# A residual graph layer on one core: the gate as w + p·d, the last weights split early, and the last row tile in two column pieces

## The chip, the core and the metric

The kernel runs on one core of a Trainium2 chip. The time is the device time of one execution in microseconds (us), and the median of the runs is compared. The engines run side by side and wait for each other by semaphores only: PE multiplies matrices, ACT and DVE work on rows of 128 partitions, POOL does so more slowly, and SP issues the DMAs.

## The reference

625 nodes with 1024 features, 20000 edges of 8 types. The first layer is a graph attention (a product with W, softmax-like weights over the edges, elu), added to x and normalized. The second layer is relational: a product with a root matrix and, per type, a product of the mean of the neighbours with that type's weights. Its result u then gates the layer:

```python
u = _rgcn(x, edge_index, edge_type, weight, root, bias)
z = jnp.concatenate([u, x], axis=1) @ w_gate + b_gate
h = jnp.tanh(u) * z + x * (1.0 - z)
return h
...
x = _layernorm(x + _L1_gnn_ref(x, ...), axis=-1)
```

With the residual, what is normalized is 2x + z·(tanh(u) − x), where z is b_gate, plus x times the lower half of w_gate, plus u times its upper half.

## The kernel before

Rows of nodes are cut into 5 row tiles of 128 (the last has 113), the 1024 features into 8 blocks k of 128 and 2 halves of 512 columns. Each product of 32-bit numbers is made of three matmuls: both operands are split into a high part (f32r) and a low rest, and hi·hi, lo·hi and hi·lo are summed in PSUM (`product_item`, L924; lines 927 to 929). A weight chunk is 128 x 512. SP loads it into a ring of four buffers `w_raw` (L294), ACT casts the high part (L459), POOL subtracts for the low part (L393). A half product, called a segment here, takes 8 chunks. The segments run in one order; `SEG_G` (22) and `SEG_G + 1` (23) are the last two, the left and right half of u times the upper half of w_gate.

Up to segment 22 the chunks are the outer loop and the row tiles the inner one, so all five tiles become ready together. Meanwhile u is turned: PE transposes it (L1119), ACT takes the high part (`turned_u`, L606) and DVE the low part (L879). Segment 23 is different: its weights are written whole into the memory of the operand `M_hi[0]`, `M_lo[0]`, which is free once segment 21 is done (`last_w`, L142). There the row tiles are the outer loop (L1140), and each tile is ready after its 24 matmuls. The names: `last_chunk(k)` is chunk k of segment 23, on ACT (L598, L602) and on POOL (L396, L398).

z holds b_gate plus the part of x already. xf is x rebuilt from its two parts, by POOL (L434). ACT makes tanh(u) in place, after each of the first five last chunks (L628). POOL subtracts xf from it (`minus_x`, L405). DVE then does, for a half of a tile (`gate`, L884): z += product in PSUM (L887), z *= u (L890), u = 2·xf + z (L891), and the statistics of the columns (L892). It does so for the five tiles of half 0, then for half 1; after a tile's half 1 it combines the statistics (L899), ACT takes the root (L631), DVE the reciprocal (L901) and the scaling (L902), and SP stores the tile (L369, L373). Most DVE instructions carry a semaphore and wait for it themselves (`step`, L639).

The order on every engine is the order in which the code is written; no scheduler moves anything. PE waits for each chunk's low part in tile 0 (L1146), and from tile 3 on for the PSUM bank that DVE has to drain (L1142).

## Time and profile before

| | |
|---|---|
| timed runs | 1111.9, 1112.72, 1115.48 us (median 1112.72) |
| profiled execution | 1117.14 us |
| its span, first to last instruction | 1115.3 us |
| busy over the span | PE 1040.4 us, DVE 353.3, ACT 264.0, POOL 265.4 |
| chain that ended last, by engine | PE 83%, DVE 7%, POOL 3% |
| loads of a weight chunk | 192 of 256 KB, 2.9 us each from issue to landing |

The busy times are sums over the whole span. The change touches only the last 75 us or so, so the profile is read there: first the stretches between the borders of segments (segment 22 from 1039.00 to 1068.49 us, segment 23 from there to 1107.26), then the timelines of single engines. The start times are us from the span's start. ACT, DVE and POOL overlap the end of an instruction with the start of the next a little. The granted clock of PE is given as a share of 2.4 GHz.

### The profile page before, as it was taken

To read this page: it belongs to the slowest core of one execution; us is meant where nothing else is said; L and a number is where in the kernel's file an instruction comes from. 1 tells how busy PE (TensorE), PEld (TensorE's weight loads), DVE (VectorE), ACT (ScalarE), POOL (GpSimd) and SP (SyncE) were. 2 spreads that over 40 slices of the span, in tenths; PEclk is the share of its full clock that TensorE was granted. 3 is DMA by queue.
4 is the path that set the end of the run, shared out by engine and by line. 5 is a ranking of instruction groups with operands and counts; after the bars stand their busy time and mean duration, and the time that the engine had idled before them with its cause. 6 is when DMAs were issued, how large, how long until landed. Compare 5 with 4: busy or idle time off the path is not lost.

```text
span 1115.3 us, 14888 instructions
## 1 busy us (share of the span) xinstructions
PE 1040.4 (93%) x5432; PEld 861.0 (77%) x5432; DVE 353.3 (32%) x698; ACT 264.0 (24%) x452; POOL 265.4 (24%) x201
## 2 busy tenths in 40 slices
PE   5699878896999999999999999999999999999977
PEld 3455545585788889889889889889889889888855
DVE  7954566446111022022022022022012012112277
ACT  3212234345111121121121121122121122222320
POOL 0000000103532222222222312321311321327480
PEclk9989989998999999999999999999999999999988
DMA  6113323425622132132131131131141141212212
GB/s 207 48 57 114 95 58 87 153 80 191 179 79 64 38 108 65 39 115 59 38 121 52 38 123 51 38 125 48 38 135 39 38 135 38 76 48 66 76 39 92
DMA packets 63621, 91.81 MB, mean 82 GB/s; under 512 B 4115, under 2 KB 30178, under 8 KB 63428
## 3 DMA queue, kind: packets, MB, share of 16 engines
q1 hardware_dynamic: 63556, 90.86, 25.8%
q8 instruction: 51, 0.84, 0.3%
q14 instruction: 14, 0.11, 0.0%
HBM read 75.17 MB, written 15.67 MB: 81 GB/s over the span
## 4 chain that ended last, share of the span: by engine, by line
PE 83%; DVE 7%; POOL 3%; issue 2%; ACT 1%; DVEq 1%; POOLq 0%; ACTq 0%
PE ps L927 17%; PE ps L928 17%; PE ps L929 17%; PE ps L1098 9%; PE ps L1099 9%; PE ps L993 4%; PE ps L1087 2%; PE ps L956 2%; DVE hot L761 2%; POOL x_lo L420 1%; PE ps L1147 1%; POOL u L405 1%; PE ps L1148 1%; PE ps L1149 1%; DVE oh_s L699 1%
## 5 line engine op out<-in xcount | busy, mean ns | idle before, releaser
L393 POOL TENSOR_TENSOR w_lo<-w_raw,w_hi 128x512 fp32r<-128x512 f32 x168 | 215.3, 1285 | 771.0 <-ACT w_hi L459 553.6
L927 PE MATMUL ps<-w_hi,M_hi 128*128 128x512 f32 (+1 forms) x560 | 223.5, 399 | 17.7 <-DVE w_lo L694 11.4
L459 ACT CAST w_hi<-w_raw 128x512 fp32r<-128x512 f32 x184 | 114.2, 622 | 480.0 <-PE ps L929 415.3
L928 PE MATMUL ps<-w_hi,M_lo 128*128 128x512 f32 (+1 forms) x560 | 220.3, 393 | 0.0
L929 PE MATMUL ps<-w_lo,M_hi 128*128 128x512 f32 (+1 forms) x560 | 220.2, 393 | 0.0
L842 DVE SCALAR_TENSOR_TENSOR u<-ps,scale,u 128x512 f32<-128x512 f32 (+1 forms) x90 | 66.4, 744 | 423.1 <-PE ps L929 423.1
L1098 PE MATMUL ps<-C_hi,x_hi 128*128 128x320 f32 (+3 forms) x640 | 193.1, 319 | 0.0
L1099 PE MATMUL ps<-C_hi,x_lo 128*128 128x320 f32 (+3 forms) x640 | 192.0, 317 | 0.0
L927 PE MATMUL ps<-w_hi,M 128*128 128x512 f32 (+1 forms) x360 | 140.5, 390 | 0.0
L929 PE MATMUL ps<-w_lo,M 128*128 128x512 f32 (+1 forms) x360 | 140.5, 390 | 0.0
L928 PE MATMUL ps<-w_hi,M 128*128 128x512 f32 (+1 forms) x360 | 140.4, 390 | 0.0
L927 PEld LDWEIGHTS ps<-w_hi,M_hi 128*128 128x128 f32 (+1 forms) x560 | 105.1, 188 | 43.2 <-DVE w_lo L694 13.6
L1099 PEld LDWEIGHTS ps<-C_hi,x_lo 128*128 128x128 f32 (+1 forms) x640 | 127.5, 199 | 0.3
L1098 PEld LDWEIGHTS ps<-C_hi,x_hi 128*128 128x128 f32 (+1 forms) x640 | 127.3, 199 | 0.4
L929 PEld LDWEIGHTS ps<-w_lo,M_hi 128*128 128x128 f32 (+1 forms) x560 | 105.0, 188 | 23.7
L928 PEld LDWEIGHTS ps<-w_hi,M_lo 128*128 128x128 f32 (+1 forms) x560 | 105.3, 188 | 22.4
L761 DVE TENSOR_SCALAR hot<-table,key 128x640 bf16<-128x640 f16 x210 | 69.9, 383 | 70.1 <-PE ps L993 53.9
L993 PE MATMUL ps<-hot,oh_s 128*128 128x320 bf16 x420 | 76.0, 313 | 13.3 <-DVE hot L761 6.3
L929 PEld LDWEIGHTS ps<-w_lo,M 128*128 128x128 f32 (+1 forms) x360 | 66.7, 185 | 14.9
L928 PEld LDWEIGHTS ps<-w_hi,M 128*128 128x128 f32 (+1 forms) x360 | 66.8, 186 | 14.6
L927 PEld LDWEIGHTS ps<-w_hi,M 128*128 128x128 f32 (+1 forms) x360 | 66.8, 185 | 14.5
L993 PEld LDWEIGHTS ps<-hot,oh_s 128*128 x420 | 31.0, 99 | 46.4 <-issue 39.1
(140 smaller groups left out, 768.8 us busy)
## 6 DMA issues: line engine op xcount, KB each, us to landing
w_raw<-weights SPq DMA_DIRECT2D x192, 256.0 KB, 2.9
C_dram<-Cst SPq DMA_DIRECT2D x25, 512.0 KB, 5.9
C_hi<-C_dram SPq DMA_DIRECT2D x8, 1600.0 KB, 6.9
z<-b_gate SPq DMA_DIRECT2D x5, 512.0 KB, 9.6
u<-bias SPq DMA_DIRECT2D x5, 512.0 KB, 8.5
xT_raw<-xT SPq DMA_DIRECT2D x8, 312.5 KB, 7.5
u<-x SPq DMA_DIRECT2D x4, 512.0 KB, 5.0
out<-u SPq DMA_DIRECT2D x4, 512.0 KB
```

The source lines that it names most:

```text
L393: pool.tensor_tensor(w_lo[k % RING][:, :], w_raw[k % RING][:, :], w_hi[k % RING][:, :].bitcast(f32), ALU.subtract).then_inc(w_lo_done, 1)
L459: nc.scalar.copy(w_hi[k % RING][:, :], w_raw[k % RING][:, :]).then_inc(w_hi_done, 1)
L761: v.tensor_scalar(hot[:, SLOT[s] * NP:(SLOT[s] + 1) * NP], table[:, :], float(WIN * w), key[:, ds(tile + s, 1)], ALU.add, ALU.is_equal).th ...
L842: v.scalar_tensor_tensor(u[r, t, half * H2:(half + 1) * H2], bank(t, rows(t)), scale[odd][r, t:t + 1], u[r, t, half * H2:(half + 1) * H2], ...
L927: mm(o, lhs_hi[:, k, c], w_hi[k % RING][:, :], start=opens, stop=False)
L928: mm(o, lhs_lo[:, k, c], w_hi[k % RING][:, :], start=False, stop=False)
L929: last = mm(o, lhs_hi[:, k, c], w_lo[k % RING][:, :], start=False, stop=closes_)
L956: last = mm(bank(turn_bank(j, part), c0=(m - m0) * P, c=P), Cst[j % 2][:, m, r, :], ident_r[:, :], start=r == 0, stop=r == R - 1)
L993: last = mm(bank(5 + c, c=SPLIT), oh_s[:, ds(edge + s * P, P)], hot[:, SLOT[s] * NP + c * SPLIT:SLOT[s] * NP + (c + 1) * SPLIT], start=Fal ...
L1087: last = mm(bank(5, c0=2 * t, c=2), C_hi[:, m, t * P:(t + 1) * P], ones_r[:, 0:2], start=m == 0, stop=m == NT - 1)
L1098: mm(o, x1_hi[r, m, f], C_hi[r, m, c0:c0 + cn], start=m == 0, stop=False)
L1099: last = mm(o, x1_lo[r, m, f], C_hi[r, m, c0:c0 + cn], start=False, stop=m == NT - 1)
```

## The change

It has three parts.

First, the gate is written as w + p·d, with p the product in PSUM, d = tanh(u) − xf and w = 2·xf + z·d. DVE makes d in place of u and w in place of z, over 1024 columns at a time and before the gate's product is there (`gate_rest`); POOL's `minus_x` is gone. What is left per half tile is one multiplication that reads PSUM and one addition, which also sums its result. In tiles 0 to 3 the variance no longer comes from `bn_stats`: DVE makes the negative mean, ACT squares the deviations over 1024 columns with a sum (z only takes the squares), and then takes the root.

Second, the last weights are loaded and split earlier. The memory of x1_lo lies now, with that of C_hi, where xf and four buffers `last_raw` come, so chunks 0 to 3 of segment 23 have their own buffers; 4 to 7 still use the ring. They have semaphores of their own, and ACT and POOL take them between the last chunks of segment 22.

Third, the last row tile is multiplied in two pieces of 256 columns into two banks. DVE treats that tile in four quarters of 256 columns with `bn_stats`.

```diff
+            with ExitStack() as agg:
+                C_hi = sb("C_hi", [P, NT, NP], f32r, agg)
+                space = sb("space", [P, NT * (D - NP)], f32, agg)
+                x1_lo = sb("x1_lo", [P, NT, D], f32r, agg)
...
             xf = sb("xf", [P, NT, D], f32, late)
+            last_raw = [sb(f"last_raw{k}", [P, H2], f32, late) for k in range(RING)]
+            space2 = sb("space2", [P, NT * D - RING * H2], f32, late)
+            u = sb("u", [P, NT, D], f32, late)
+            z = sb("z", [P, NT, D], f32, late)
+            x1_hi = sb("x1_hi", [P, NT, D], f32r, late)
...
+        def raw_of_last(k):
+            return (last_raw[k] if k < RING else w_raw[k % RING])[:, :]
...
-            for n in range(SEG_U + 2 * R, SEG_G + 2):
-                load_ahead(n, last=n == SEG_G + 1)
+            for n in range(SEG_U + 2 * R, SEG_G + 1):
+                load_ahead(n, last=n == SEG_G)
+            sp.wait_ge(xf_done, NT)
+            for k in range(KT):
+                if k >= RING:
+                    sp.wait_ge(w_lo_done, 8 * SEG_G + k + 1)
+                r0, c0 = chunk_rows(SEG_G + 1, k)
+                sp.dma_start(raw_of_last(k), weights[ds(r0, P), c0:c0 + H2]).then_inc(last_here[k], 16)
...
             def last_chunk(k):
-                pool.wait_ge(w_hi_done, 8 * (SEG_G + 1) + k + 1)
-                pool.tensor_tensor(last_w(1, k), w_raw[k % RING][:, :], last_w(0, k).bitcast(f32),
-                                   ALU.subtract).then_inc(w_lo_done, 1)
-
-            def minus_x(t):
-                r = slice(0, rows(t))
-                pool.wait_ge(tanh_done, t + 1)
-                pool.wait_ge(xf_done, t + 1)
-                pool.tensor_tensor(u[r, t, :], u[r, t, :], xf[r, t, :], ALU.subtract).then_inc(d_done, 1)
+                pool.wait_ge(last_hi_done, k + 1)
+                pool.tensor_tensor(last_w(1, k), raw_of_last(k), last_w(0, k).bitcast(f32),
+                                   ALU.subtract).then_inc(last_lo_done, 1)
...
-            for k in range(KT):
-                if k < RING:
-                    split_chunk(SEG_G, k + RING)
-                else:
-                    last_chunk(k - RING)
-                if k >= KT - NT:
-                    minus_x(k - KT + NT)
-            for k in range(RING, KT):
+            split_chunk(SEG_G, RING)
+            last_chunk(0)
+            split_chunk(SEG_G, RING + 1)
+            last_chunk(1)
+            split_chunk(SEG_G, RING + 2)
+            last_chunk(2)
+            last_chunk(3)
+            split_chunk(SEG_G, RING + 3)
+            for k in range(4, KT):
                 last_chunk(k)
...
-                act.wait_ge(raw_here[k % RING], 32 * (SEG_G + 1) + 16 * (k // RING) + 16)
+                act.wait_ge(last_here[k], 16)
                 if k == 0:
                     act.wait_ge(u_ready, filled(SEG_G - 1))
-                nc.scalar.copy(last_w(0, k), w_raw[k % RING][:, :]).then_inc(w_hi_done, 1)
+                nc.scalar.copy(last_w(0, k), raw_of_last(k)).then_inc(last_hi_done, 1)
+
+            def tanh(t):
+                nc.scalar.activation(u[0:rows(t), t, :], u[0:rows(t), t, :], ACT.Tanh).then_inc(tanh_done, 1)
...
-            for kh in range(2):
-                n = SEG_G - 1 + kh
-                split_chunk(n, RING)
-                for t in range(GB):
-                    turned_u(t, kh)
-                split_chunk(n, RING + 1)
-                for t in range(GB, NT):
-                    turned_u(t, kh)
-                for k in range(RING + 2, KT):
-                    split_chunk(n, k)
-                if kh == 0:
-                    for k in range(RING):
-                        split_chunk(n + 1, k)
-            for k in range(KT):
+            split_chunk(SEG_G - 1, RING)
+            for t in range(GB):
+                turned_u(t, 0)
+            split_chunk(SEG_G - 1, RING + 1)
+            for t in range(GB, NT):
+                turned_u(t, 0)
+            for k in range(RING + 2, KT):
+                split_chunk(SEG_G - 1, k)
+            for k in range(RING + 1):
+                split_chunk(SEG_G, k)
+            for t in range(GB):
+                turned_u(t, 1)
+            last_chunk(0)
+            split_chunk(SEG_G, RING + 1)
+            for t in range(GB, NT):
+                turned_u(t, 1)
+            last_chunk(1)
+            tanh(0)
+            tanh(1)
+            split_chunk(SEG_G, RING + 2)
+            last_chunk(2)
+            tanh(2)
+            last_chunk(3)
+            tanh(3)
+            split_chunk(SEG_G, RING + 3)
+            last_chunk(4)
+            tanh(4)
+            for k in range(5, KT):
                 last_chunk(k)
-                if k < NT:
-                    act.wait_ge(uT_lo_done, 2 * NT)
-                    nc.scalar.activation(u[0:rows(k), k, :], u[0:rows(k), k, :], ACT.Tanh).then_inc(tanh_done, 1)
-            for t in range(NT):
-                act.wait_ge(var_done, t + 1)
-                nc.scalar.activation(rstd[0:rows(t), t:t + 1], mv[0:rows(t), t, 1:2], ACT.Sqrt,
-                                     bias=eps_col[0:rows(t), :]).then_inc(std2_done, 1)
+            for t in range(NT - 1):
+                r = slice(0, rows(t))
+                act.wait_ge(h_mean_done, t + 1)
+                nc.scalar.activation(z[r, t, :], u[r, t, :], ACT.Square, bias=h_neg_mean[r, t:t + 1],
+                                     accum_out=h_sq[r, t:t + 1]).then_inc(h_sq_done, 1)
+                act.wait_ge(h_sq_done, t + 1)
+                nc.scalar.activation(rstd[r, t:t + 1], h_sq[r, t:t + 1], ACT.Sqrt, bias=eps_col[r, :], scale=1.0 / D)\
+                  .then_inc(std2_done, 1)
+            r = slice(0, rows(NT - 1))
+            act.wait_ge(var_done, 1)
+            nc.scalar.activation(rstd[r, NT - 1:NT], mv[r, NT - 1, 1:2], ACT.Sqrt, bias=eps_col[r, :]).then_inc(std2_done, 1)
...
+            def gate_rest(t):
+                r = slice(0, rows(t))
+                dve.wait_ge(tanh_done, t + 1)
+                dve.wait_ge(xf_done, t + 1)
+                step(v.tensor_tensor(u[r, t, :], u[r, t, :], xf[r, t, :], ALU.subtract))
+                step(v.tensor_tensor(z[r, t, :], z[r, t, :], u[r, t, :], ALU.mult))
+                step(v.scalar_tensor_tensor(z[r, t, :], xf[r, t, :], 2.0, z[r, t, :], ALU.mult, ALU.add))
+
             def gate(t, half, from_bank):
                 r, c = slice(0, rows(t)), slice(half * H2, (half + 1) * H2)
                 dve.wait_ge(u_ready, NT * (SEG_G + half) + t + 1)
-                v.tensor_tensor(z[r, t, c], bank(from_bank, rows(t)), z[r, t, c], ALU.add).then_inc(u_drained, 1)
+                v.tensor_tensor(u[r, t, c], bank(from_bank, rows(t)), u[r, t, c], ALU.mult).then_inc(u_drained, 1)
                 dve.wait_ge(u_drained, NT * (SEG_G + half) + t + 1 + NT)
-                dve.wait_ge(d_done, t + 1)
-                step(v.tensor_tensor(z[r, t, c], z[r, t, c], u[r, t, c], ALU.mult))
-                step(v.scalar_tensor_tensor(u[r, t, c], xf[r, t, c], 2.0, z[r, t, c], ALU.mult, ALU.add))
-                step(v.bn_stats(stats[r, t, half, :], u[r, t, c]))
+                step(v.scalar_tensor_tensor(u[r, t, c], u[r, t, c], 1.0, z[r, t, c], ALU.mult, ALU.add,
+                                            accum_out=h_sum[r, t, half:half + 1]))
+
+            quarters = stats[:, 0:2, :, :].rearrange("p a b s -> p (a b) s")
+
+            def gate_quarter(q, from_bank, from_col):
+                t = NT - 1
+                r, c = slice(0, rows(t)), slice(q * Q, (q + 1) * Q)
+                at = NT * SEG_G + NT if q < 2 else NT * SEG_G + 2 * NT + q - 2
+                dve.wait_ge(u_ready, at)
+                step(v.tensor_tensor(u[r, t, c], bank(from_bank, rows(t), c0=from_col, c=Q), u[r, t, c], ALU.mult))
+                step(v.tensor_tensor(u[r, t, c], u[r, t, c], z[r, t, c], ALU.add))
+                step(v.bn_stats(quarters[r, q, :], u[r, t, c]))
+
+            def normalized(t, mean, op):
+                r = slice(0, rows(t))
+                dve.wait_ge(std2_done, t + 1)
+                step(v.reciprocal(rstd[r, t:t + 1], rstd[r, t:t + 1]))
+                v.tensor_scalar(u[r, t, :], u[r, t, :], mean, rstd[r, t:t + 1], op, ALU.mult).then_inc(y2_done, 1)
 
             for t in range(NT):
+                gate_rest(t)
+            for t in range(NT - 1):
                 gate(t, 0, t)
-            for t in range(NT):
+            for q in range(2):
+                gate_quarter(q, NT - 1, q * Q)
+            dve.sem_inc(u_drained, 1)
+            for t in range(NT - 1):
                 r = slice(0, rows(t))
                 gate(t, 1, last_bank(t))
-                v.bn_aggr(mv[r, t, :], stats[r, t, :, :]).then_inc(var_done, 1)
-                dve.wait_ge(std2_done, t + 1)
-                step(v.reciprocal(rstd[r, t:t + 1], rstd[r, t:t + 1]))
-                v.tensor_scalar(u[r, t, :], u[r, t, :], mv[r, t, 0:1], rstd[r, t:t + 1], ALU.subtract, ALU.mult)\
-                    .then_inc(y2_done, 1)
+                v.tensor_scalar(h_neg_mean[r, t:t + 1], h_sum[r, t, 1:2], h_sum[r, t, 0:1], -1.0 / D, ALU.add, ALU.mult)\
+                 .then_inc(h_mean_done, 1)
+                normalized(t, h_neg_mean[r, t:t + 1], ALU.add)
+            r = slice(0, rows(NT - 1))
+            for q in range(2, 4):
+                gate_quarter(q, last_bank(NT - 1) + q - 2, 0)
+            v.bn_aggr(mv[r, NT - 1, :], quarters[r, :, :]).then_inc(var_done, 1)
+            normalized(NT - 1, mv[r, NT - 1, 0:1], ALU.subtract)
...
-                c, o = slice(t * P, t * P + rows(t)), bank(last_bank(t), rows(t))
-                for k in range(KT):
-                    if t == 0:
-                        pe.wait_ge(w_lo_done, 8 * (SEG_G + 1) + k + 1)
-                    mm(o, M_hi[1][:, k, c], last_w(0, k), start=k == 0, stop=False)
-                    mm(o, M_lo[1][:, k, c], last_w(0, k), start=False, stop=False)
-                    last = mm(o, M_hi[1][:, k, c], last_w(1, k), start=False, stop=k == KT - 1)
-                last.then_inc(u_ready, 1)
+                c = slice(t * P, t * P + rows(t))
+                pieces = [(0, H2)] if t < NT - 1 else [(0, Q), (Q, H2)]
+                for f0, f1 in pieces:
+                    if f0 > 0:
+                        pe.wait_ge(u_drained, NT * SEG_G + t - GB + 2 + NT)
+                    o = bank(last_bank(t) + (f0 > 0), rows(t), c=f1 - f0)
+                    for k in range(KT):
+                        if t == 0:
+                            pe.wait_ge(last_lo_done, k + 1)
+                        mm(o, M_hi[1][:, k, c], last_w(0, k)[:, f0:f1], start=k == 0, stop=False)
+                        mm(o, M_lo[1][:, k, c], last_w(0, k)[:, f0:f1], start=False, stop=False)
+                        last = mm(o, M_hi[1][:, k, c], last_w(1, k)[:, f0:f1], start=False, stop=k == KT - 1)
+                    last.then_inc(u_ready, 1)
```

**ACT around the last chunks.** Before; w_hi is a chunk of segment 22, M_hi<-w_raw a last chunk, M<-ps a turned tile of u:

```order
289 L459 CAST w_hi<-w_raw 128x512 [waits w_used,raw_here1]
290 L606 CAST M<-ps 128x4x128 [waits uT_ready]
291 L606 CAST M<-ps 128x4x113 [waits uT_ready]
292 L459 CAST w_hi<-w_raw 128x512 [waits w_used,raw_here2]
293 L459 CAST w_hi<-w_raw 128x512 [waits w_used,raw_here3]
294 L602 CAST M_hi<-w_raw 128x512 [waits u_ready,raw_here0]
295 L628 ACT_TABLE_LOAD
296 L628 ACTIVATE u<-u 128x1024 [waits uT_lo_done]
```

and after the change:

```order
289 L617 CAST M_hi<-last_raw 128x512 [waits u_ready,last_here0]
290 L474 CAST w_hi<-w_raw 128x512 [waits w_used,raw_here1]
291 L624 CAST M<-ps 128x4x128 [waits uT_ready]
292 L624 CAST M<-ps 128x4x113 [waits uT_ready]
293 L617 CAST M_hi<-last_raw 128x512 [waits last_here1]
294 L620 ACT_TABLE_LOAD
295 L620 ACTIVATE u<-u 128x1024 x2
296 L474 CAST w_hi<-w_raw 128x512 [waits w_used,raw_here2]
297 L617 CAST M_hi<-last_raw 128x512 [waits last_here2]
```

The table load and the first tanh stood behind all of segment 22's chunks and stand now behind chunk 5, ahead of chunk 6.

**POOL around the last chunks.** Before; w_lo is a chunk of segment 22, M_lo a last chunk:

```order
96 L393 TENSOR_TENSOR w_lo<-w_raw,w_hi 128x512 [waits w_hi_done] x7
97 L405 TENSOR_TENSOR u<-u,xf 128x1024 [waits xf_done,tanh_done]
98 L398 TENSOR_TENSOR M_lo<-w_raw,M_hi 128x512 [waits w_hi_done]
99 L405 TENSOR_TENSOR u<-u,xf 128x1024 [waits xf_done,tanh_done]
100 L398 TENSOR_TENSOR M_lo<-w_raw,M_hi 128x512 [waits w_hi_done]
101 L405 TENSOR_TENSOR u<-u,xf 128x1024 [waits xf_done,tanh_done]
102 L398 TENSOR_TENSOR M_lo<-w_raw,M_hi 128x512 [waits w_hi_done]
```

and after:

```order
97 L418 TENSOR_TENSOR M_lo<-last_raw,M_hi 128x512 [waits last_hi_done]
98 L413 TENSOR_TENSOR w_lo<-w_raw,w_hi 128x512 [waits w_hi_done]
99 L418 TENSOR_TENSOR M_lo<-last_raw,M_hi 128x512 [waits last_hi_done]
100 L413 TENSOR_TENSOR w_lo<-w_raw,w_hi 128x512 [waits w_hi_done]
101 L418 TENSOR_TENSOR M_lo<-last_raw,M_hi 128x512 [waits last_hi_done] x2
102 L413 TENSOR_TENSOR w_lo<-w_raw,w_hi 128x512 [waits w_hi_done]
103 L418 TENSOR_TENSOR M_lo<-w_raw,M_hi 128x512 [waits last_hi_done] x4
```

The last chunks stand now between those of segment 22, and the subtractions of xf are gone.

**DVE in one row tile of half 1.** Before:

```order
901 L887 TENSOR_TENSOR z<-ps,z 128x512 [waits u_ready,dve_step]
902 L890 TENSOR_TENSOR z<-z,u 128x512 [waits d_done,u_drained]
903 L891 SCALAR_TENSOR_TENSOR u<-xf,z 128x512 [waits dve_step]
904 L892 BN_STATS stats<-u 128x6 [waits dve_step]
905 L899 BN_AGGR mv<-stats 128x2 [waits dve_step]
906 L901 RECIPROCAL rstd<-rstd 128x1 [waits std2_done]
907 L902 TENSOR_SCALAR u<-u,mv,rstd 128x1024 [waits dve_step]
```

and after, with the three instructions that each tile now has ahead of all gates:

```order
881 L924 TENSOR_TENSOR u<-u,xf 128x1024 [waits xf_done,tanh_done]
882 L925 TENSOR_TENSOR z<-z,u 128x1024 [waits dve_step]
883 L926 SCALAR_TENSOR_TENSOR z<-xf,z 128x1024 [waits dve_step]
```

```order
910 L931 TENSOR_TENSOR u<-ps,u 128x512 [waits dve_step,u_ready]
911 L933 SCALAR_TENSOR_TENSOR u,h_sum<-u,z 128x512 [waits u_drained]
912 L963 TENSOR_SCALAR h_neg_mean<-h_sum 128x1 [waits dve_step]
913 L950 RECIPROCAL rstd<-rstd 128x1 [waits std2_done]
914 L951 TENSOR_SCALAR u<-u,h_neg_mean,rstd 128x1024 [waits dve_step]
```

Two operations and `bn_stats` have left the round; the reciprocal waits as before for ACT's root, which has now a Square ahead of it:

```order
307 L661 ACTIVATE z,h_sq<-u,h_neg_mean 128x1024 [waits h_mean_done]
308 L664 ACT_TABLE_LOAD
309 L664 ACTIVATE rstd<-h_sq,eps_col 128x1 [waits h_sq_done]
310 L661 ACTIVATE z,h_sq<-u,h_neg_mean 128x1024 [waits h_mean_done]
311 L664 ACTIVATE rstd<-h_sq,eps_col 128x1 [waits h_sq_done]
```

## Rows read from the trace of the kernel before

**Rows 1.** Stretches: us, then busy of PE, PEld, DVE, ACT, POOL, PEclk, DMA share, GB/s.

```profile
1039.00:1068.49 29.49, 29.49 (x141) 24.34 (x141) 6.61 (x9) 14.35 (x21) 16.23 (x11) 1.00 0.23 71
1068.49:1085.50 17.01, 9.94 (x27) 6.01 (x26) 16.50 (x16) 3.14 (x4) 15.04 (x8) 0.70 0.11 33
1085.50:1107.26 21.76, 21.76 (x96) 17.41 (x94) 17.75 (x32) 1.18 (x4) 0.00 (x0) 1.00 0.18 74
```

**Rows 2.** Timeline of PE: start, duration, engine, instruction, idle before and its releaser.

```profile
1074.55 0.50 PE L1147 MATMUL ps<-M_hi,M 128*128 128x512 f32 x1 [3.45 <-POOL M_lo L398]
...
1078.99 0.80 PE L1147 MATMUL ps<-M_hi,M 128*128 128x512 f32 x1 [3.47 <-POOL M_lo L398]
```

**Rows 3.** Timeline of DVE, row tile 0 of the second half.

```profile
1087.75 0.69 DVE L887 TENSOR_TENSOR z<-ps,z 128x512 f32<-128x512 f32 x1
...
1090.66 0.21 DVE L899 BATCH_NORM_AGGREGATE mv<-stats 128x2 f32<-128x12 f32 x1
1091.23 0.17 DVE L901 RECIPROCAL rstd<-rstd 128x1 f32<-128x1 f32 x1 [0.36 <-ACT rstd L631]
...
1092.16 0.68 DVE L887 TENSOR_TENSOR z<-ps,z 128x512 f32<-128x512 f32 x1
```

**Rows 4.** Timeline of all engines, the end of the program.

```profile
1110.20 0.21 DVE L899 BATCH_NORM_AGGREGATE mv<-stats 113x2 f32<-113x12 f32 x1
...
1110.98 0.81 DVE L902 TENSOR_SCALAR u<-u,mv,rstd 113x1024 f32<-113x1024 f32 x1
1111.82 0.67 SPq L373 DMA_DIRECT2D out<-u  x2
```

**Rows 5.** Timeline of ACT, from the last turning of u to tanh.

```profile
1048.01 1.02 ACT L606 CAST M<-ps 128x512 fp32r<-128x512 f32 x2
1051.74 0.62 ACT L459 CAST w_hi<-w_raw 128x512 fp32r<-128x512 f32 x1 [2.72 <-PE ps L929]
...
1055.67 0.62 ACT L602 CAST M_hi<-w_raw 128x512 fp32r<-128x512 f32 x1
1056.30 1.28 ACT L628 ACT_TABLE_LOAD   x1
1057.60 1.06 ACT L628 ACTIVATE u<-u 128x1024 f32<-128x1024 f32 x1
...
1059.07 1.05 ACT L628 ACTIVATE u<-u 128x1024 f32<-128x1024 f32 x1
```

**Rows 6.** Timeline of POOL, alone and then beside DVE.

```profile
1055.84 1.29 POOL L393 TENSOR_TENSOR w_lo<-w_raw,w_hi 128x512 fp32r<-128x512 f32 x1 [2.11 <-ACT w_hi L459]
...
1065.97 2.39 POOL L405 TENSOR_TENSOR u<-u,xf 128x1024 f32<-128x1024 f32 x1
1068.33 1.74 POOL L398 TENSOR_TENSOR M_lo<-w_raw,M_hi 128x512 fp32r<-128x512 f32 x1
1070.03 2.80 POOL L405 TENSOR_TENSOR u<-u,xf 128x1024 f32<-128x1024 f32 x1
```

**Rows 7.** Timeline of DVE over the same stretch.

```profile
1066.70 2.21 DVE L890 TENSOR_TENSOR z<-z,u 128x512 f32<-128x512 f32 x1
1068.94 1.67 DVE L891 SCALAR_TENSOR_TENSOR u<-xf,z 128x512 f32<-128x512 f32 x1
...
1071.38 0.69 DVE L887 TENSOR_TENSOR z<-ps,z 128x512 f32<-128x512 f32 x1
1072.10 1.27 DVE L890 TENSOR_TENSOR z<-z,u 128x512 f32<-128x512 f32 x1
```

**Rows 8.** DVE groups by line and form: busy us, mean ns, idle before.

```profile
L855 DVE TENSOR_TENSOR M_lo<-ps,M_hi 128x306 fp32r<-128x306 f32 x32 | 15.3, 477 | 21.0 <-ACT M_hi L587 21.0
...
L724 DVE SCALAR_TENSOR_TENSOR M<-ps,a_bc 128x512 fp32r<-128x512 f32 x8 | 5.2, 685 | 0.1
...
L797 DVE SCALAR_TENSOR_TENSOR u<-gt,u 128x1024 f32<-128x1024 f32 x4 | 4.9, 1225 | 0.1
...
L724 DVE DVE_READ_ACCUMULATOR M<-ps,a_bc 128x1 f32 x8 | 0.6, 80 | 0.0
```

More of the change, by code:

```diff
@@ L78, in gat_rgcn_kernel @@
         stats = sb("stats", [P, NT, 2, 6], f32)
+        h_sum = sb("h_sum", [P, NT, 2], f32)
+        h_sq = sb("h_sq", [P, NT], f32)
+        h_neg_mean = sb("h_neg_mean", [P, NT], f32)
         dots = sb("dots", [P, 4 * NT], f32)
@@ L128, in gat_rgcn_kernel @@
         with ExitStack() as late:
-            x1_hi = sb("x1_hi", [P, NT, D], f32r, late)
-            x1_lo = sb("x1_lo", [P, NT, D], f32r, late)
-            u = sb("u", [P, NT, D], f32, late)
-            z = sb("z", [P, NT, D], f32, late)
+            with ExitStack() as agg:
+                C_hi = sb("C_hi", [P, NT, NP], f32r, agg)
+                space = sb("space", [P, NT * (D - NP)], f32, agg)
+                x1_lo = sb("x1_lo", [P, NT, D], f32r, agg)
             with ExitStack() as elu:
@@ L135, in gat_rgcn_kernel @@
                 et = [sb(f"et{b}", [P, D], f32, elu) for b in range(2)]
-            with ExitStack() as agg:
-                C_hi = sb("C_hi", [P, NT, NP], f32r, agg)
             xf = sb("xf", [P, NT, D], f32, late)
+            last_raw = [sb(f"last_raw{k}", [P, H2], f32, late) for k in range(RING)]
[3 more added lines that the diff above has]
+            x1_hi = sb("x1_hi", [P, NT, D], f32r, late)
         g_parts = [m[:, :, :].rearrange("p a b -> p (a b)") for m in (M_hi[0], M_lo[0])]
@@ L233, in gat_rgcn_kernel @@
         xf_done = sem("xf_done")
-        d_done = sem("d_done")
+        last_here = [sem(f"last_here{k}") for k in range(KT)]
+        last_hi_done = sem("last_hi_done")
+        last_lo_done = sem("last_lo_done")
+        h_mean_done = sem("h_mean_done")
+        h_sq_done = sem("h_sq_done")
         var_done = sem("var_done")
@@ L257, in gat_rgcn_kernel @@
         EARLY = 2 * NT
+        Q = H2 // 2
         ALL = KT * NT
```

## Prediction

> **What bounds the kernel now.** I first split the end of the span into stretches [rows 1]. From 1039.00 to 1068.49 us, the product of the first gate half, PE has no idle time and the granted clock is 1.00 (2.4 GHz). In the next 17.01 us PE is busy only 9.94 us, the clock is 0.70, while POOL is busy 15.04 and DVE 16.50. From 1085.50 to 1107.26 PE is again full at 1.00. The last product has 120 matmuls; at the pace of the last stretch, 21.76 us for 96, that is 0.227 us each, it would take 27.2 us without gaps. It takes 38.77. PE's own timeline names the loss [rows 2]: 3.45 and 3.47 us of idle time, both ended by POOL's low part of a late chunk, and the matmul behind the second reads 0.80 us where the one behind the first read 0.50. So 11.5 us look free on PE.
>
> Next I looked at who finishes last if PE does not, and that is DVE. Its second-half rounds [rows 3] go from 1087.75 to 1092.16, 4.4 us a tile, with one wait on ACT of 0.36 us, and the first ones start as soon as half 0 is through. Of the 11.5 us, only what DVE can also give back shows at the end. From DVE's last instruction to the end there is a fixed piece: it ends at 1111.79, the stores go out at 1111.82, the span ends at 1115.3 [rows 4]. I therefore follow DVE alone.
>
> **The change, part by part.**
>
> Start of the new work. ACT ends the turning of u at 1049.03 (1048.01 + 1.02) [rows 5]. Behind it now stand one last_chunk cast (0.62), the table load (1.28) and tanh(0) (1.06): 1052.05. DVE can start gate_rest then; it has only 6.61 us of work in 1039 to 1068 [rows 1]. tanh(1) starts 0.97 later. A tanh follows the one before it by 1.47 with a cast between [rows 5], faster than DVE's three operations per tile, so tanh is not late. The split of chunk 6 of half 0, started at 1051.74 before, now queues behind tanh(1) and reaches POOL at about 1053.6.
>
> gate_rest. It adds 15 DVE operations of 1024 columns with two SBUF inputs. The like of them takes 1.225 us [rows 8], 1.255 with the gap behind it: 18.8 us. In place of them go POOL's five subtractions of 2.4 us, and DVE's L890 and L891 halves.
>
> The price of sharing. DVE and POOL do not run such operations side by side. DVE's product issued at 1066.70 ended at 1068.91, 0.55 after POOL's ended at 1068.36; POOL's next, begun 1068.33, ended 1070.07, 1.16 after DVE's; DVE's next ended 0.54 after that [rows 6, 7]. They take turns, each waiting for the other's whole operation. An operation with one PSUM input is untouched: 0.69 at 1071.38 while POOL runs. Alone, a 512-column DVE operation takes 0.69, so 0.15 of it overlaps; a 1024-column one then needs 1.07 of its turn, a POOL chunk of 1.29 [rows 6] needs 1.14. A round is 2.21 us against 1.255 alone: 0.95 lost by DVE per POOL chunk. From 1053.6 POOL has eight chunks: chunks 6 and 7 of half 0, and last_chunk(2) to (7). Their casts come 0.5 to 1.1 us apart and are ahead of the 2.21 us rounds. Loss 7.6 us. DVE ends gate_rest at 1052.05 + 18.8 + 7.6 = 1078.45.
>
> The Trainium skill has the same sharing as a bare statement (GPSIMD Engine Reference, Key points: contention with VectorE instructions that have two SBUF inputs), without a price; the price above is this trace's.
>
> Do POOL's rounds make PE late? They end at 1053.6 + n x 2.2. Chunk 7 of half 0 is the fourth: 1062.4; PE wants it 15 matmuls (3.40 us) before 1068.49, at 1065.1. Last_chunk(7) is the eighth: 1071.2. Its load waits for that fourth one, lands 2.9 us later (65.3) and is cast by 66; PE wants it at 1068.49 + 7 x 0.68 = 1073.2. Slacks are 2.7 and 2.0 us. So PE runs through: 96 full matmuls to 1090.3, then 48 of 256 columns. Those are not in the trace; between half of 0.227 and all of it, the end is 1095.7 to 1101.2. DVE comes to the last tile later than either (below), so this part is worth nothing and costs nothing. The PSUM banks are no new wait: tile 3 wants bank 0 at 1084.8 and DVE drains it at 1079.2.
>
> SP. The loads of last 0 to 3 stand behind xf_done and chunk (half 0, 7), out at 1041.3. Five loads in flight instead of one may triple the 2.9 us; ACT's cast of last 0 may slip from 1044.8 to some 1047.5, still before its next split at 1047.48. Cost 0. The outputs wait behind nothing new.
>
> Half 0. gate is now two operations, the second with an accumulator. With one PSUM input such an operation read 685 ns and its accumulator read 82 ns, which starts at 0.61 of the main one [rows 8], so I take 0.73 a piece: four tiles x 1.455 = 5.8, to 1084.3. The quarters have six operations of 256 columns. Bounds: 0.165 us (a one-column operation such as L901) [rows 3], and 0.477 for 306 columns [rows 8]. By these two, 0.43, with gap 0.465: 2.8, to 1087.05. Before, DVE's half 0 ended at 1087.75 [rows 3]. Only 0.7 us won so far: the work has moved ahead and paid for it in turns.
>
> Half 1, tiles 0 to 3. gate 1.455, the mean 0.17. Then the new wait on ACT: a Square of 1024 columns, with tanh's 1.06 [rows 5] as the nearest row, the accumulator read, between 0 and the 0.29 of a one-column ACT operation, taken 0.15, then the root 0.29 and two handovers of 0.035: 1.57 in all against 0.36 of idle before. Behind the waiting reciprocal stands everything of DVE, the next tile's gate too; it runs in the same order as before. Then reciprocal 0.20 and the scaling 0.725. Sum 4.12 a tile against 4.40. Two operations and bn_stats went (1.5), a wait of 1.2 came. On tile 0 the root's table load, which lay hidden in ACT's idle time, stands behind the first Square: 1.29 [rows 5]. So 5.4 + 3 x 4.12 = 17.8, to 1104.85.
>
> Here the table load read 1.28 us and tanh started 0.02 behind it. The Trainium skill (ScalarE: Activation LUTs, What ACT_TABLE_LOAD costs) counts 1.38 us of drain with it, about 2.66 a switch. By the page the sum would be 1.4 us later; I go by the row.
>
> Last tile. Both pieces lie ready, DVE does both: six operations of 0.465, 2.8; then aggregate to scaled result 1.59 as before (1110.20 to 1111.79) [rows 4]. End 1109.2 against 1111.79. Gain 2.6 us.
>
> The profiled execution took 1117.14 us, more than each of the three timed runs (median 1112.72, highest 1115.48); by it the new time would be 1114.5. I take the same 2.6 us off the median, as nothing in the tail shows why it should differ there. By the median: **1110.1 us**.
>
> **Rivals.**
>
> Taking turns costs less than I say (B). The eight turns are read from operations of 512 columns on DVE. If long ones are not held, or POOL waits instead, DVE keeps 7.6 us: 1102.5. The turn-taking fits every pair in the rows to 0.02 us; that is against it. For it: no 1024-column pair stands there.
>
> The time follows PE (D). What the gaps alone suggest: PE ends at about 1096.3, then 1.4 and 1.6 us on DVE: 12.5 us less, 1100.2. It needs DVE to arrive at the last tile 8.5 us earlier than summed; even B's 7.6 is not enough. Against it is the DVE share of 16.50 in 17.01 us.
>
> The accumulator halves DVE (C), the slower side. All eight gate additions now read two f32 SBUF tensors and accumulate. Place: L933 of the changed kernel, on DVE's path in both halves. At twice the streaming part, 0.54 more each, it costs 4.3 us and the time is 1114.4, above before. It decides the sign once such an operation takes over 1.02 us. For it: no row shows two SBUF inputs with an accumulator. Against it: without one, 1225 ns for 1024 columns, and with one and a PSUM input 685 for 512, both the plain rate [rows 8]. The Trainium skill (Vector Engine (DVE) Microarchitecture Reference, Points that are easy to get wrong) says that this form with two non-bf16 SBUF sources halves throughput, as no port is left for the accumulator; L797 contradicts it as far as it goes without an accumulator.
>
> The change does not do what it says (E): the late chunks still stop PE. With 2.0 us of slack for the last one, a slip would cost PE the clock too, as in [rows 2]; but PE has 8.5 us in hand against DVE at the last tile, so the time stays.
>
> **How the numbers follow.** Forecast with E 0.68, B 0.12, C 0.12, D 0.04, something not seen 0.04. The forecast's own range is 1108 to 1112.5: Square, accumulator and quarter operations at their bounds move it by 1.5 either way, the page's drain by 1.4 up. To hold 8 in 10 I take 1107.0 to 1114.5, which takes in C and leaves out B and D. A difference under 0.3% (3.3 us) is about what a measurement of this kernel cannot tell from none. Faster by more means under 1109.4: B, D and three tenths of the forecast, 0.36. Slower by more means above 1116.1: a quarter of C and half of the unseen, 0.05. Same 0.59.
>
> **What would show it.** PE without gaps and at clock 1.00 from 1068 to about 1096, then over ten us before DVE's end. In 1053 to 1072, DVE's 1024-column operations at about 2.2 us and POOL's chunks at the same pitch; behind it 1.22. DVE's gate_rest ends near 1078, half 0 near 1087. DVE idle for some 1.5 us per tile before the reciprocal, 2.8 on tile 0. L933 at 0.69; 1.2 means C. If DVE shows idle time ahead of L931 or L943 released by PE, DVE does not bound and the forecast is wrong.

## The result

The changed kernel is slower. Its first four runs have a median of 1123.12 us against 1112.31 for the kernel before, a ratio of 1.009 with a 95% interval of 1.0064 to 1.0116; twelve later runs gave 1120.84, 1.0062 (1.0041 to 1.0084). The forecast was 1110.1, range 1107.0 to 1114.5.

Much of the scatter between runs goes with the mean granted clock of a run, the profiler's figure for PE. Over 97 runs of the kernel before, a clock lower by 0.001 goes with 0.73 us more, and what is left scatters by 1.1 us; one more run, at a clock of 0.556, took 1736.29 us and is left out. "At equal clock" below means how far the mean time of some runs lies off this line. The change comes out 4.6 us slower at equal clock in the twelve runs, and 6.6 in the first four.

The profiled execution, at 1119.22 us the fastest of the first four, shows two things that must be kept apart: what became of the tail, and what came before it. First the stretches of segment 22 and segment 23, which answer to [rows 1]; the columns are the same:

```profile
1042.80:1072.37 29.57, 29.57 (x139) 23.96 (x138) 20.34 (x16) 15.78 (x24) 21.42 (x12) 1.00 0.29 89
1072.37:1100.10 27.73, 27.73 (x140) 23.18 (x140) 22.17 (x35) 4.36 (x7) 2.77 (x2) 1.00 0.05 19
```

Neither stretch has a gap, and the granted clock stays at 1.00. The second stretch was cut a little early at both ends: the first and the last matmul of segment 23 are these:

```profile
1072.90 0.39 PE L1219 MATMUL ps<-M_hi,M 128*128 128x512 f32 x1
...
1100.85 0.28 PE L1221 MATMUL ps<-M_lo,M 128*113 128x256 f32 x1
```

Segment 23 takes 28.2 us (1072.90 to 1101.13) where it took 38.8, so the weights' part of the change does what it says. But DVE ends at 1113.89, the stores follow at 1113.92 as in [rows 4], and the first stretch begins 3.8 us later than it did:

```profile
1113.08 0.81 DVE L951 TENSOR_SCALAR u<-u,mv,rstd 113x1024 f32<-113x1024 f32 x1
1113.92 0.67 SPq L393 DMA_DIRECT2D out<-u  x2
```

Before the change, DVE did wait for PE ahead of the last two row tiles, 1.77 us in all:

```profile
1101.86 0.69 DVE L887 TENSOR_TENSOR z<-ps,z 128x512 f32<-128x512 f32 x1 [0.82 <-PE ps L1149]
...
1107.30 0.69 DVE L887 TENSOR_TENSOR z<-ps,z 113x512 f32<-113x512 f32 x1 [0.95 <-PE ps L1149]
```

These two waits are gone now.

DVE's timeline in gate_rest, which answers to [rows 7], and POOL's beside it, to [rows 6]:

```profile
1055.83 1.23 DVE L924 TENSOR_TENSOR u<-u,xf 128x1024 f32<-128x1024 f32 x1 [2.10 <-ACT u L620]
1057.09 1.23 DVE L925 TENSOR_TENSOR z<-z,u 128x1024 f32<-128x1024 f32 x1
1058.35 2.21 DVE L926 SCALAR_TENSOR_TENSOR z<-xf,z 128x1024 f32<-128x1024 f32 x1
1060.60 2.21 DVE L924 TENSOR_TENSOR u<-u,xf 128x1024 f32<-128x1024 f32 x1
...
1074.02 2.20 DVE L924 TENSOR_TENSOR u<-u,xf 128x1024 f32<-128x1024 f32 x1
1076.26 1.23 DVE L925 TENSOR_TENSOR z<-z,u 128x1024 f32<-128x1024 f32 x1
```

```profile
1057.33 2.15 POOL L413 TENSOR_TENSOR w_lo<-w_raw,w_hi 128x512 fp32r<-128x512 f32 x1 [2.17 <-ACT w_hi L474]
...
1063.92 2.28 POOL L413 TENSOR_TENSOR w_lo<-w_raw,w_hi 128x512 fp32r<-128x512 f32 x1
1066.16 8.99 POOL L418 TENSOR_TENSOR M_lo<-w_raw,M_hi 128x512 fp32r<-128x512 f32 x4
```

The same kind of operation takes 1.23 us alone and 2.20 to 2.21 while POOL has chunks, eight times in a row; POOL's four last chunks take 8.99 us; at the 1.29 us of one alone [rows 6] it would be 5.2. DVE leaves gate_rest at 1082.56.

Then a row tile of half 1, the answer to [rows 3], first DVE, then ACT:

```profile
1092.74 0.21 DVE L963 TENSOR_SCALAR h_neg_mean<-h_sum 128x1 f32<-128x1 f32 x1
1095.88 0.17 DVE L950 RECIPROCAL rstd<-rstd 128x1 f32<-128x1 f32 x1 [2.92 <-ACT rstd L664]
...
1096.81 0.68 DVE L931 TENSOR_TENSOR u<-ps,u 128x512 f32<-128x512 f32 x1
...
1100.11 0.16 DVE L950 RECIPROCAL rstd<-rstd 128x1 f32<-128x1 f32 x1 [1.64 <-ACT rstd L664]
...
1101.04 0.68 DVE L931 TENSOR_TENSOR u<-ps,u 128x512 f32<-128x512 f32 x1
```

```profile
1092.99 1.15 ACT L661 ACTIVATE z<-u,h_neg_mean 128x1024 f32<-128x1024 f32 x1 [23.45 <-DVE h_neg_mean L963]
1094.05 0.19 ACT L661 ACTIVATION_READ_ACCUMULATOR z<-u,h_neg_mean 128x1 f32 x1
1094.25 1.28 ACT L664 ACT_TABLE_LOAD   x1
1095.55 0.29 ACT L664 ACTIVATE rstd<-h_sq,eps_col 128x1 f32<-128x1 f32 x1
```

DVE waits 2.92 us on tile 0 and 1.64 on the next; a round is 4.23 us (1096.81 to 1101.04). ACT's Square takes 1.15, its accumulator read 0.19, the table load 1.28, the root 0.29.

From the start of the last drains of segment 21 (DVE copies its products out of PSUM, 1036.54 before, 1040.29 after) to DVE's last result it is 75.25 us before and 73.60 after: the tail gained 1.65 us. This is one pair of profiles. In the seven of the kernel before and its padded forms below, the same stretch reads 74.66 to 75.25, in the five of the changed kernel and its moved forms 73.39 to 73.60. What lies ahead of those drains lost 3.75 in this pair. Matmuls show where. ACT casts a chunk each time PE has gone through 15 matmuls, so the start of the casts gives PE's pace. In the second relation, where the stationary operand lies in M1, before:

```profile
422.88 0.62 ACT L459 CAST w_hi<-w_raw 128x512 fp32r<-128x512 f32 x1 [2.78 <-PE ps L929]
426.28 0.62 ACT L459 CAST w_hi<-w_raw 128x512 fp32r<-128x512 f32 x1 [2.78 <-PE ps L929]
429.68 0.62 ACT L459 CAST w_hi<-w_raw 128x512 fp32r<-128x512 f32 x1 [2.78 <-PE ps L929]
```

and after:

```profile
422.89 0.62 ACT L474 CAST w_hi<-w_raw 128x512 fp32r<-128x512 f32 x1 [2.86 <-PE ps L996]
426.37 0.62 ACT L474 CAST w_hi<-w_raw 128x512 fp32r<-128x512 f32 x1 [2.86 <-PE ps L996]
429.85 0.62 ACT L474 CAST w_hi<-w_raw 128x512 fp32r<-128x512 f32 x1 [2.86 <-PE ps L996]
```

3.40 us a chunk has become 3.48: 0.227 us a matmul is 0.232. The order of the program is the same there, and from 405 to 434 us the granted clock is 1.00 in both traces, so the clock is not the cause. It is so in all products whose stationary operand is in M1 (relations 1, 3, 5, 7 counted from 0, and segments 22 and 23; 1200 matmuls, of which the changed kernel has the last 24 as 48 narrow ones), and in none that multiplies M_hi0 and M_lo0 by a chunk of weights. 1200 times 5.3 ns is 6.4 us; 960 of them, 5.1 us, lie ahead of the tail, of which this one pair shows 3.75. The 150 matmuls of the first layer that have M_hi0 or M_lo0 as the stationary and M1 as the moving operand (L1031 to L1033) are slower too, a median of 0.232 us from start to start for 0.227, some 0.6 us more.

### The profile page after: what moved, and what is told of

Same layout as the page of the kernel before. It is cut to its first block, busy times and chain, and to the rows that moved or that the text cites. A ratio compares the mean times of both kernels' runs of the same rounds, so it can differ in the third digit from the quotient of the medians.

```text
span 1117.4 us, 14943 instructions
## 1 busy us (share of the span) xinstructions
PE 1041.8 (93%) x5456; PEld 860.2 (77%) x5456; DVE 360.7 (32%) x709; ACT 268.7 (24%) x460; POOL 259.2 (23%) x196
## 4 chain that ended last, share of the span: by engine, by line
PE 79%; DVE 10%; issue 2%; ACT 2%; POOL 1%; DVEq 1%; DMA 0%; SPq 0%; ACTq 0%
PE ps L994 17%; PE ps L996 17%; PE ps L995 17%; PE ps L1165 9%; PE ps L1166 9%; PE ps L1060 4%; PE ps L1023 2%; PE ps L1154 2%; DVE hot L797 2%; POOL x_lo L434 1%; DVE u L924 1%; DVE z L926 1%; DVE z L925 1%; DVE oh_s L735 1%; PE ps L1031 1%
## 5 line engine op out<-in xcount | busy, mean ns | idle before, releaser
L413 POOL TENSOR_TENSOR w_lo<-w_raw,w_hi 128x512 fp32r<-128x512 f32 x168 | 218.0, 1301 | 764.0 <-ACT w_hi L474 549.1
```

Source lines behind the costliest of these rows:

```text
L413: pool.tensor_tensor(w_lo[k % RING][:, :], w_raw[k % RING][:, :], w_hi[k % RING][:, :].bitcast(f32), ALU.subtract).then_inc(w_lo_done, 1)
```

## Experiments

The three small tiles that the change adds (h_sum, h_sq, h_neg_mean) take 128 bytes of each partition and are allocated ahead of M1. M1 moved from byte 85632 to 85760. The chunks w_raw, w_hi and w_lo start at 57472, 65664 and 73856, M_hi0 and M_lo0 at 16512 and 36992. All these but the new M1 are 128 above a multiple of 256. The ratio given with each run is to the kernel before on the same chip, with its 95% interval; the pace is the mean distance of the matmuls' starts in the odd relations, in us.

### The place of M1

```diff
         stats = sb("stats", [P, NT, 2, 6], f32)
+        pad = sb("pad", [P, 32], f32)
         dots = sb("dots", [P, 4 * NT], f32)
```

> The kernel before with one unused tile of 128 bytes a partition ahead of dots, so that dots, key, table, M1 and all behind it lie 128 bytes higher, as in the changed kernel; nothing else. Theory P (place): the products whose stationary operand lies in M1 go at 0.232 us a matmul instead of 0.227, in the odd relations and in the last two segments of the program, 1200 matmuls, 6.4 us: about 1119, and up to 1123 if the place explains the whole loss of the changed kernel. Theory C (the changed code slows it): 1112, all matmuls at 0.227.

Measured: 1119.81 us, 1.0064 (1.0042 to 1.0086), pace 0.2321, all even relations 0.2268. An unused tile of 128 bytes makes the kernel before 7 us slower. The instructions are the same, so the changed code has no part in it. At equal clock it is 6.0 us.

```diff
-        h_sum = sb("h_sum", [P, NT, 2], f32)
-        h_sq = sb("h_sq", [P, NT], f32)
-        h_neg_mean = sb("h_neg_mean", [P, NT], f32)
...
             x1_hi = sb("x1_hi", [P, NT, D], f32r, late)
+            h_sum = sb("h_sum", [P, NT, 2], f32, late)
+            h_sq = sb("h_sq", [P, NT], f32, late)
+            h_neg_mean = sb("h_neg_mean", [P, NT], f32, late)
```

> The changed kernel with h_sum, h_sq and h_neg_mean allocated last, above x1_hi, so that M1 and all behind it lie where they did before; instructions unchanged. Theory P: matmuls back at 0.227 us, and only the tail's own gain is left: segment 21's drain to the last scaling takes 73.6 us instead of 75.25, about 1110.5 to 1111. Theory C: 1121 to 1123, as the changed kernel.

Measured: 1110.44 us, 0.9988 (0.997 to 1.0006), pace 0.227, tail 73.39 us. With M1 left alone the change can't be told from the kernel before. The median lies 0.3 us from the forecast's 1110.1, which is no proof of the sum: the interval is 4 us wide, and the tail gained less than was forecast (below).

With the same tiles directly behind M1:

> The changed kernel with the three small tiles allocated behind M1: M1, dots, key and table lie as before the change, and what comes behind M1 (oh_s, Cst, C_hi, x1, u, z, xf) is 128 bytes higher. Theory P, if it is M1's place alone: 1110.5 to 1111, matmuls at 0.227. If what lies behind M1 counts: between 1112 and 1123, and its trace shows which lines are slower. Theory C: 1121 to 1123.

Measured: 1113.01 us, 1.0008 (0.9991 to 1.0025), pace 0.2268. M1's own place is what counts. The 2.6 us between this and the run before go with the clock, 0.971 on average here and 0.974 there: at equal clock this one is 2.0 us below the kernel before and that one 1.2, and the tail reads 73.43.

With a pad of 256 bytes in the kernel before (64 floats in the first diff):

> The kernel before with 256 unused bytes ahead of dots: M1 starts at 85888, 128 above a multiple of 256 as before the change, but at another place in 512. Theory P with a rule by 256 bytes: 1112, matmuls at 0.227. Theory P with a rule by 512 bytes (stationary and moving operand at one place of 512): 1119 or more, M1's matmuls at about 0.232. Theory C: 1112.

Measured: 1112.87 us, 0.9997 (0.998 to 1.0015), pace 0.2271. So moving by 128 bytes costs and moving by 256 does not. Whose place? The next two move the other operand:

```diff
+        pad = sb("pad", [P, 32], f32)
         w_raw = [sb(f"w_raw{b}", [P, H2], f32) for b in range(RING)]
...
+        pad2 = sb("pad2", [P, 32], f32)
         dots = sb("dots", [P, 4 * NT], f32)
```

> The kernel before with 128 unused bytes ahead of w_raw and 128 ahead of dots: the chunks of weights w_raw, w_hi, w_lo start at multiples of 256 bytes, M_hi0 and M_lo0 stay where they were, M1 lies 256 higher, and both M still start 128 above a multiple of 256. Theory R (the place of the stationary operand against that of the moving one decides): now every product of the loop has the pair that was slow, all matmuls of it at 0.232 us, some 2500 of them slower by 5 ns, 13 us: 1125. Theory A (the stationary operand's own place decides): all at 0.227, 1112.6.

Measured: 1126.87 us, 1.0118 (1.0084 to 1.0151), pace 0.2321 in odd and even relations. ACT's casts, in the same relation as above:

```profile
422.40 0.62 ACT L461 CAST w_hi<-w_raw 128x512 fp32r<-128x512 f32 x1 [2.86 <-PE ps L931]
425.88 0.62 ACT L461 CAST w_hi<-w_raw 128x512 fp32r<-128x512 f32 x1 [2.86 <-PE ps L931]
429.37 0.62 ACT L461 CAST w_hi<-w_raw 128x512 fp32r<-128x512 f32 x1 [2.86 <-PE ps L931]
```

3.48 us again, though neither M is at a new place in 256. Segment 23 of this same run settles it from the other side. Its weights lie in M_hi0 and M_lo0, which were not moved, so both operands are again 128 above a multiple of 256, and its matmuls start every 0.227 us, where those of segment 22 just before it start every 0.232 to 0.233.

```diff
+        pad = sb("pad", [P, 32], f32)
         M_hi = [sb("M_hi0", [P, KT, NP], f32r)]
```

> The kernel before with 128 unused bytes ahead of M_hi0, so that M0, the chunks of weights and M1 all start at multiples of 256 bytes. Theory R: all pairs are alike again, matmuls at 0.227 us, 1112.6. Theory A: the products of both M at 0.232, about 1125.

Measured: 1113.13 us, 0.9998 (0.9979 to 1.0018), pace 0.2270 everywhere:

```profile
421.22 0.62 ACT L460 CAST w_hi<-w_raw 128x512 fp32r<-128x512 f32 x1 [2.78 <-PE ps L930]
424.62 0.62 ACT L460 CAST w_hi<-w_raw 128x512 fp32r<-128x512 f32 x1 [2.78 <-PE ps L930]
428.02 0.62 ACT L460 CAST w_hi<-w_raw 128x512 fp32r<-128x512 f32 x1 [2.78 <-PE ps L930]
```

All operands at multiples of 256 are as fast as all at 128 above one. It is the difference of the two places that costs. How large the difference must be was asked with 64 and 32 bytes in the first diff:

> The kernel before with 64 unused bytes ahead of dots: M1 starts 64 bytes off the weights' chunks, counted in 256. If any difference between the two operands' places in 256 bytes costs, M1's matmuls go at about 0.232 and the time is near 1119. If only a difference of 128 (an exact half) does, 0.227 and 1112.6.

> The same with 32 bytes. Any difference costs: 0.232, near 1119. Only whole multiples of 128 count: 0.227, 1112.6.

Measured: 1123.77 us, 1.0093 (1.0061 to 1.0125), pace 0.2328 with 64 bytes; 1118.59 us, 1.0042 (1.0018 to 1.0066), pace 0.2325 with 32. Each difference tried (32, 64, 128) costs 5 to 6 ns a matmul in these products. The two times differ by 5 us though the paces do not: the mean clocks were 0.967 and 0.974, and at equal clock the two pads cost 6.4 and 6.0 us. The 150 matmuls of the first layer, where M1 is the moving operand, make one exception: their median is 0.233 us with 32 bytes and 0.232 with 128, but 0.229 with 64. It stays open.

Last, the changed kernel as it stands with 128 bytes more ahead of dots, and the changed kernel again:

> The changed kernel, all tiles where they are in it, with 128 more unused bytes ahead of dots, so that M1 is 256 higher than before the change and again at the weights' place in 256. If the place of M1 is the whole cause, this one more pad takes the loss away: matmuls at 0.227, tail 73.5, 1110.4. If the changed order of the code or the new places behind M1 cost: 1113 or more.

> The changed kernel once more, for more runs of it. The place of M1 and the tail together make it the 1119.8 of before_pad128 less the tail's 1.6 to 2.2 us: 1117.6 to 1118.2. Only its first four runs (median 1123.1) speak for more; if it stays at 1122 or above, some 4 us of it have another cause than those two.

Measured: 1111.83 us, 0.9986 (0.9967 to 1.0004), pace 0.227, tail 73.40, for the first; 1120.84, 1.0062 (1.0041 to 1.0084), pace 0.2321, tail 73.58, for the second. One more unused tile takes the loss away and leaves the code's own result, found twice, at 0.9988 and 0.9986. The expectation for the second, 1117.6 to 1118.2, was missed by 2.6 us or more, and its mean clock was low, 0.970. At equal clock it is 4.6 us slower than the kernel before, and the sum of the parts is 6.0 for the place of M1 less 1.2 to 2.0 for the tail (after_h_last, after_h_behind_m1, after_plus128), 4.0 to 4.8. The first four runs, at 6.6 by the same line, lie some 2 us above that; no run shows why.

### The tail

All runs of this part have the three small tiles allocated last, so that M1 lies where it did before; the tail to compare with is the 73.39 us of after_h_last.

```diff
             def last_chunk(k):
                 pool.wait_ge(last_hi_done, k + 1)
-                pool.tensor_tensor(last_w(1, k), raw_of_last(k), last_w(0, k).bitcast(f32),
+                c = slice(0, H2 if k < 2 else 8)
+                pool.tensor_tensor(last_w(1, k)[:, c], raw_of_last(k)[:, c], last_w(0, k)[:, c].bitcast(f32),
...
-                        last = mm(o, M_hi[1][:, k, c], last_w(1, k)[:, f0:f1], start=False, stop=k == KT - 1)
+                        last = mm(o, M_hi[1][:, k, c], last_w(int(k < 2), k)[:, f0:f1], start=False, stop=k == KT - 1)
```

> The changed kernel with M1 in its old place. It leaves out most of the low part of chunks 2 to 7 of the last weights: POOL makes 8 columns of each instead of 512, and the third matmul takes the high part for them. Theory T (DVE and POOL take turns at operations with two SBUF inputs): in gate_rest only the two chunks of segment 22 cost a full turn, so five or six of the ten slow DVE operations of 2.2 us fall to 1.2 to 1.5, gate_rest is 4 to 5.6 us shorter, and so is the program. Rival (the 1024-column operations are slow for another cause, such as the DMA loads or ACT's tanh): the 2.2 us stay as long as ACT and the loads run.

Measured: a single execution, 1107.8 us; tail 67.69 us against 73.39. The kernel leaves out most of the low part of six chunks, so its output is not the layer's, and only its timeline is used. DVE's timeline, the third to the seventh operation of gate_rest, and POOL's at the same time:

```profile
1052.55 2.20 DVE L927 SCALAR_TENSOR_TENSOR z<-xf,z 128x1024 f32<-128x1024 f32 x1
1054.79 1.27 DVE L925 TENSOR_TENSOR u<-u,xf 128x1024 f32<-128x1024 f32 x1
1056.09 2.21 DVE L926 TENSOR_TENSOR z<-z,u 128x1024 f32<-128x1024 f32 x1
1058.34 1.27 DVE L927 SCALAR_TENSOR_TENSOR z<-xf,z 128x1024 f32<-128x1024 f32 x1
1059.64 1.23 DVE L925 TENSOR_TENSOR u<-u,xf 128x1024 f32<-128x1024 f32 x1
```

```profile
1051.53 2.13 POOL L413 TENSOR_TENSOR w_lo<-w_raw,w_hi 128x512 fp32r<-128x512 f32 x1 [2.09 <-ACT w_hi L475]
1053.64 1.34 POOL L419 TENSOR_TENSOR M_lo<-last_raw,M_hi 128x8 fp32r<-128x8 f32 x2
1054.99 2.23 POOL L413 TENSOR_TENSOR w_lo<-w_raw,w_hi 128x512 fp32r<-128x512 f32 x1
1057.18 2.48 POOL L419 TENSOR_TENSOR M_lo<-w_raw,M_hi 128x8 fp32r<-128x8 f32 x3
```

Only the two operations that meet a full chunk take 2.2 us; beside one of 8 columns it is 1.27. ACT and the loads are not the cause: the operation at 1054.79 took 1.27 us while ACT ran its last tanh (1055.34 to 1056.39) and the ring's loads were still under way (until 1057.58). The gain is 5.7 us for six chunks, 0.95 each: taking turns with POOL is the cause.

```diff
                  .then_inc(h_mean_done, 1)
-                normalized(t, h_neg_mean[r, t:t + 1], ALU.add)
+                if t > 0:
+                    normalized(t - 1, h_neg_mean[:, t - 1:t], ALU.add)
...
             v.bn_aggr(mv[r, NT - 1, :], quarters[r, :, :]).then_inc(var_done, 1)
+            normalized(NT - 2, h_neg_mean[:, NT - 2:NT - 1], ALU.add)
```

> The changed kernel with the small tiles allocated last (M1 in its old place), and DVE's reciprocal and scaling of a tile issued one tile later, behind the next tile's gate, in the second half. Theory D (DVE alone sets the end): the waits on ACT of 2.92 and three times 1.64 us shrink to some 1.2 in all, the tail is 6.8 us shorter, the time 1103.6. If PE or the stores set the end instead: little less than 1110.4.

Measured: 1105.33 us, 0.9925 (0.9898 to 0.9952), tail 66.13 us, 7.3 less. PE and the loads are as they were, so DVE's own chain sets the end. The time lies 1.7 us above the expected 1103.6, which was counted from the 1110.4 of after_h_last on another chip, though the tail shrank by 0.5 us more than expected; at equal clock it is 6.8 us below the kernel before, and after_h_last 1.2.

Without the column pieces (the edit told in words), `pieces = [(0, H2)]` for all tiles and multiply, add, bn_stats on 512 columns:

> The changed kernel with M1 in its old place and without the column pieces: the last row tile's product is one product of 512 columns, and DVE does it in halves of 512 (multiply, add, bn_stats). Theory D (DVE alone sets the end): three operations of 0.73 in place of six of 0.46, 0.58 us less in each half, 1.2 us in all, 1109.2 against 1110.4. Rival (the pieces bring the end forward, as PE's end is awaited): 1 to 2 us slower than 1110.4.

Measured: 1109.81 us, 0.9968 (0.995 to 0.9986), tail 72.20, 1.19 less as expected. The pieces cost what they add on DVE.

With bn_stats, bn_aggr and the root of the variance for all tiles, in place of the sum, the mean and the squares on ACT:

> The changed kernel with M1 in its old place and with bn_stats, bn_aggr and the root of the variance for all row tiles; gate as w + p*d and the rest as changed. Theory D: half 0 gets 2.9 us longer (four times 0.73), half 1 gets 3.1 shorter (3.77 a tile for 4.23 and 5.53), so about 1110.2, no difference from 1110.4: the squares on ACT were worth nothing. Rival (taking the statistics off DVE is what gains): 1113 or more.

Measured: 1111.43 us, 0.9989 (0.9968 to 1.001), tail 72.79, 0.6 less. DVE waits 0.36 us a tile again:

```profile
1087.07 0.16 DVE L941 RECIPROCAL rstd<-rstd 128x1 f32<-128x1 f32 x1 [0.36 <-ACT rstd L659]
...
1090.74 0.16 DVE L941 RECIPROCAL rstd<-rstd 128x1 f32<-128x1 f32 x1 [0.36 <-ACT rstd L659]
```

So the squares on ACT won nothing as they were placed. The rivals of the last two runs (1 to 2 us slower without the pieces, 2.5 us or more slower with bn_stats) are out by the tails, which both became shorter; the times alone, with intervals of 4 us, would not show it.

Both edits together, the scaling one tile later and no column pieces:

> Both: scaling of a tile behind the next tile's gate, and no column pieces, M1 in its old place. Theory D: 1105.3 less 1.2, so 1104.1; the fastest of all.

Measured: 1101.85 us, 0.9897 (0.9868 to 0.9926): the fastest, 1.0% below the kernel before. It is 2.2 us under the expectation, at the highest mean clock of all runs (0.978). Tail 64.93 us, 1.2 less than with skew alone, as expected. In DVE's timeline of half 1 one wait is left, and the later reciprocals find their roots ready:

```profile
1088.69 0.16 DVE L947 RECIPROCAL rstd<-rstd 128x1 f32<-128x1 f32 x1 [1.34 <-ACT rstd L664]
...
1091.21 0.15 DVE L947 RECIPROCAL rstd<-rstd 128x1 f32<-128x1 f32 x1
...
1093.71 0.15 DVE L947 RECIPROCAL rstd<-rstd 128x1 f32<-128x1 f32 x1
```

## Why the prediction was wrong

**The step that failed** is the one that opened the sum: "I therefore follow DVE alone", with the work ahead of 1039 us left at what it was. The part-by-part count has no line for the three added tiles, and the text ahead of it says that the change touches only the last 75 us or so. That holds for the instructions and not for the memory: the tiles issue nothing, but they move M1 by 128 bytes, and 1200 matmuls then take 0.232 us in place of 0.227. Measured alone it is 0.64% (0.42 to 0.86), 7.2 us, or 6.0 at equal clock. Less the tail's 1.2 to 2.0 us that gives 4.0 to 4.8, and the twelve later runs show 4.6. None of the rivals was near it; it fell under "something not seen", at 0.04. The last step, "I take the same 2.6 us off the median", is where the error enters the number: it takes a gain of the tail for a gain of the whole. All sizes below are against the tail's own start.

**What bounds the tail** was right: PE runs through at clock 1.00 and ends 12.8 us before DVE's last result. The 11.5 us of gaps on PE came back as 10.5 in segment 23 (38.8 less 28.2), and at the end only what DVE could give back came. D, the time that follows PE, is out.

**The tail's sum** was 2.6 us of gain; 1.65 came. Its terms:

| term | forecast, us | measured, us |
|---|---|---|
| last drain of segment 21 to the start of gate_rest | 15.5 | 15.54 |
| gate_rest | 26.4 | 26.73 |
| half 0 | 8.6 | 8.72 |
| half 1, tiles 0 to 3 | 17.8 | 18.23 |
| last tile | 4.4 | 4.38 |

(The first forecast term is 1052.05 less 1036.54.) The error of 0.95 us is spread: 0.3 in gate_rest, 0.15 that DVE idles between the halves for its own bn_stats, and 0.43 in half 1. Of the last, 0.27 are DVE's waits on ACT, 2.92 and three times 1.64 or 1.63 for 2.86 and 1.57 (Square read 1.15 and not 1.06 and its accumulator read 0.19 and not 0.15), and the rest is the mean, 0.21 and not 0.17. The prediction says that two operations and bn_stats went from a round; it is one operation and bn_stats, four of 0.73 us having become two, and the 1.5 us that it takes for them fit that. The cast of last 0 slipped to 1050.67 by 2.0 us of waiting for the load, and cost nothing, as said. A round of turns was forecast at 2.21 and read 2.23 to 2.25 from start to start, which is most of the 0.3; the eight came.

**B** is out by the same rows, and pool_narrow shows that the turns are the cause. **C** is out: the accumulating addition (L933) reads 0.69 us for 512 columns with two f32 inputs in SBUF, as L890 did without an accumulator, and 0.08 for the read, and the sentence of the Trainium skill (Vector Engine (DVE) Microarchitecture Reference, Points that are easy to get wrong) on halved throughput does not hold for it here. **The table load** cost 1.28 and the root began 0.02 later (1094.25 to 1095.55), so the 2.66 of the Trainium skill (ScalarE: Activation LUTs, What ACT_TABLE_LOAD costs) was not paid on this path either. **E** did not come up: the late chunks were in time.
